# Moving the second expert stretch ahead of the last two head pairs, and spreading the VectorE side jobs over the cycles

## The reference

```
x = x + attn_a(layernorm(x))   # 16 heads of 16, ALiBi bias, causal, biases on q, k, v, o
x = x + ffn(layernorm(x))      # dropless experts, 8 experts, top 2
x = x + attn_b(layernorm(x))   # 16 heads of 16, rotary q and k, causal
x = x + ffn(layernorm(x))      # the same experts and the same routing
```

## Time and profile before

| what | value |
|---|---|
| time, median of 3 runs | 4382.41 us (4375.72 to 4391.83) |
| time of the profiled execution | 4379.86 us |
| its span, first to last instruction | 4378.1 us |
| mean granted TensorE clock | 0.967 |
| TensorE matmul busy | 4043.3 us, 92% |
| VectorE busy | 2996.7 us, 68% |
| ScalarE busy | 2815.2 us, 64% |
| GpSimd busy | 816.2 us, 19% |
| DMA, mean | 93 GB/s |

### The profile page before, as it was taken

How to read it: one execution, slowest core, us unless ns; L and a number is a source line. 1 busy time by engine, 2 the same in 40 slices (tenths; PEclk the granted TensorE clock), 3 DMA queues, 4 the chain that set the end, 5 groups by cost and what they waited for, 6 DMA issues and landing times.

```text
span 4378.1 us, 107651 instructions
## 1 busy us (share of the span) xinstructions
PE 4043.3 (92%) x42369; PEld 2482.4 (57%) x42369; DVE 2996.7 (68%) x3995; ACT 2815.2 (64%) x5843; POOL 816.2 (19%) x832
## 2 busy tenths in 40 slices
PE   5899999999999999998999999999999999998875
PEld 4455555555555555557855555555555555554764
DVE  4888887878877777880078888788888777773000
ACT  2377777777777776672257777777777777667211
POOL 3000001111111122330032222222232320111012
PEclk9799999999999999999989999999999999999987
DMA  5222233233333433335543333323423232221553
GB/s 175 49 61 61 61 78 80 64 77 98 75 72 77 106 83 91 96 90 178 189 110 94 86 87 99 93 72 91 113 75 92 76 90 57 59 56 61 160 172 116
DMA packets 247476, 407.05 MB, mean 93 GB/s; under 512 B 29325, under 2 KB 162189, under 8 KB 233869
## 3 DMA queue, kind: packets, MB, share of 16 engines
q1 hardware_dynamic: 243896, 391.76, 34.0%
q0 software_dynamic: 3072, 8.39, 0.6%
HBM read 264.25 MB, written 121.50 MB: 88 GB/s over the span
## 4 chain that ended last, share of the span: by engine, by line
PE 44%; DVE 5%; ACT 3%; issue 3%; DMA 2%; POOL 1%; SPq 0%; ACTq 0%; DVEq 0%; POOLq 0%
PE ps_acc L909 11%; PE ps_r L848 8%; PE ps_p L878 7%; PE ps_r L1001 5%; PE ps_p L990 4%; DVE part_max L1122 4%; ACT probs L730 3%; PE ps_r L948 2%; PE ps_r L956 2%; PE ps_r L952 1%; PE ps_r L853 1%; DMA hid_f<-rows_by_expert 1%; PE ps_p L872 1%; PE ps_p L885 0%; DVE xl L1083 0%
## 5 line engine op out<-in xcount | busy, mean ns | idle before, releaser
L1122 DVE TENSOR_REDUCE part_max<-ps_p 128x2 f32<-128x1024 f32 (+3 forms) x2560 | 2624.2, 1060 | 716.6 <-PE ps_p L878 530.2
L730 ACT ACTIVATE probs<-ps_r 128x512 f32<-128x512 f32 (+1 forms) x4608 | 2348.0, 574 | 724.4 <-PE ps_r L848 451.7
L848 PE MATMUL ps_r<-q_stack,k_stack 54*128 54x512 f32 (+3 forms) x5120 | 1381.2, 392 | 30.9 <-ACT probs L730 15.7
L878 PE MATMUL ps_p<-k_stack,q_stack 52*128 52x512 f32 (+3 forms) x5120 | 1243.1, 434 | 90.8 <-DVE part_max L1122 71.2
L909 PE MATMUL ps_acc<-probs,v_head 128*17 128x256 f32 x19456 | 1159.5, 364 | 1.2 <-ACT probs L730 1.2
L848 PEld LDWEIGHTS ps_r<-q_stack,k_stack 54*128 54x128 f32 x5120 | 733.5, 189 | 243.2 <-ACT probs L730 182.4
L878 PEld LDWEIGHTS ps_p<-k_stack,q_stack 52*128 52x128 f32 x5120 | 556.6, 189 | 418.1 <-DVE part_max L1122 237.4
L909 PEld LDWEIGHTS ps_acc<-probs,v_head 128*17 128x17 f32 x19456 | 492.5, 98 | 477.4 <-issue 226.3
L1198 DVE COPY xf<-ps_r 128x256 f32<-128x256 f32 x60 | 25.5, 424 | 460.0 <-PE ps_r L1001 460.0
L948 PE MATMUL ps_r<-xT,wqkv 128*128 128x256 f32 x1024 | 289.6, 409 | 17.4 <-ACT probs L730 14.5
L853 PE MATMUL ps_r<-id,mk 64*128 64x64 bf16 x3584 | 280.3, 195 | 0.0
(11 more groups left out here) (94 smaller groups left out, 2301.8 us busy)
## 6 DMA issues: line engine op xcount, KB each, us to landing
probs<-w_dram SPq DMA_DIRECT2D x60, 1024.0 KB, 8.3
q_stack<-parts SPq DMA_DIRECT2D x384, 128.0 KB
k_stack<-parts SPq DMA_DIRECT2D x384, 128.0 KB
parts<-pa SPq DMA_DIRECT2D x128, 256.0 KB, 2.5
parts<-pb SPq DMA_DIRECT2D x128, 256.0 KB, 3.5
o_sums<-acc_sb SPq DMA_DIRECT2D x1024, 17.0 KB
bk<-o_sums SPq DMA_DIRECT2D x64, 256.0 KB
bk<-recips SPq DMA_DIRECT2D x64, 256.0 KB
```

Source lines behind the costliest of these rows:

```text
L730: act.activation(probs[:, at % PBUF, u, 0:w], block_bank(g, n, u)[:, 0:w], ACT.Exp)\
L848: mm = pe.matmul(bank[:, col:col + QW - q0], ks[s][r, kb * P:(kb + 1) * P], qs[s][r, qt * QW + q0:(qt + 1) * QW], start=fresh, stop=True, ...
L878: mm[u] = pe.matmul(banks[:, u, col:col + w], qs[s][r, qb * P:(qb + 1) * P], ks[s][r, kc * QW:kc * QW + w], start=fresh, stop=True, skip_g ...
L1122: mm = dve.tensor_reduce(part_max[:, :, qb, kc], ps_p[:, p1_banks(g, n), col:col + w], AX_X, ALU.max)
```

## The change

The change has five parts. The second expert stretch is moved from behind pair 63 to behind pair 61 (`EX_AFTER`). The projection of batch 6, whose routed rows the stretch needs, is moved to earlier cycles of pairs 56 to 62 (`Y_ALONE`). The first two tiles' rows and the first tile's W1 are loaded already at step 30 of the pair before each stretch, W1 into the free buffer of the rows to be mixed (`first_rows`, `w1_first`); those rows are loaded later instead. Norm parts `ln` stand at the last step of a cycle, one per cycle; the mixing becomes 16 jobs, one per cycle from step 11 of the pair behind a stretch. The last batch is projected by query tile: jobs `zl` to `zo` load row sums, invert, store them, load, scale, project into `ps_p` and add on VectorE, for tile 3 inside pair 63, for tiles 2, 1 and 0 behind it. `AFTER_AT` and `AFTER_SP` go.

```diff
+Y_ALONE = (8, 11, 14, 17, 23, 26, 29, 32, 37, 39, 41, 43, 49, 51, 53, 55)
+EX_AFTER = (NG // 2 - 1, NG - 3)
+LAST = NB - 1
...
-        return [(t, ("ld", f, c, 0))] + [(t + 7 + 2 * i, ("ln", f, c, i)) for i in range(len(NORM_FROM))]
+        first = CYCLE * ((t + 7) // CYCLE) + CYCLE - 1
+        return [(t, ("ld", f, c, 0))] + [(first + CYCLE * i, ("ln", f, c, i)) for i in range(len(NORM_FROM))]
...
-            y_at = [slot_step(k) for k in Y_SLOTS[CH * c:CH * (c + 1)]]
+            y_at = [slot_step(k) for k in (Y_SLOTS if f is not None else Y_ALONE)[CH * c:CH * (c + 1)]]
...
-    if g == NG // 2:
-        for n, k in ((26, 0), (30, 1)):
-            steps[n].append(("fm", 0, 0, k))
-        steps[31].append(("fo", 0, 0, 0))
+    for ly in range(2):
+        for i in range(TOPK * NFT):
+            at = MIX_STEP + CYCLE * i
+            if g == EX_AFTER[ly] + 1 + at // STEPS:
+                steps[at % STEPS].append(("fm", ly, 0, i))
+    if g == EX_AFTER[0] + 2:
+        steps[STEPS - 1].append(("fo", 0, 0, 0))
+    if g == EX_AFTER[0] or g == EX_AFTER[1]:
+        steps[FETCH_STEP].append(("xw", EX_AFTER.index(g), 0, 0))
+    if g == NG - 1:
+        for n, job in LAST_JOBS:
+            steps[n].append(job)
...
+MIX_STEP, FETCH_STEP = 11, 30
+LAST_JOBS = ((19, ("zl", 3, 0)), (20, ("zc", 3, 0)), (20, ("zs", 3, 0)), (21, ("zb", 3, 0)), (22, ("zx", 3, 0)),
+             (23, ("zm", 3, 0)), (28, ("z", 3, 0)), (28, ("z", 3, 1)), (29, ("zl", 2, 0)), (30, ("zc", 2, 0)),
+             (30, ("zs", 2, 0)), (31, ("zb", 2, 0)), (31, ("zm", 2, 0)), (32, ("z", 3, 2)), (32, ("z", 3, 3)),
+             (34, ("za", 3, 0)), (34, ("za", 3, 1)), (34, ("za", 3, 2)), (34, ("za", 3, 3)), (34, ("zx", 2, 0)),
+             (35, ("zl", 1, 0)), (35, ("zc", 1, 0)))
...
+                elif kind == "zb":
...
+                    sp.dma_start(z_rows[c], rows_of(x_a, b, c)).then_inc(z_in[c], 16)
+                    for k in range(KD):
+                        sp.dma_start(z_o[c][:, k, :], o_d[f % 2, k * PAIRS:(k + 1) * PAIRS, 0:DH, cols]).then_inc(z_in[c], 16)
+                    sp.wait_ge(z_recip_st, 16 * (NQ - c))
+                    for k in range(KD):
+                        r = r_d[f % 2, k * PAIRS:(k + 1) * PAIRS, cols].rearrange("h (o n) -> h o n", o=1)
+                        sp.dma_start(z_rl[c][:, k, :], r.broadcast_to([PAIRS, DH, QW])).then_inc(z_in[c], 16)
...
+            def first_rows(ly):
...
+                for i in range(2):
+                    sp.dma_start(xs_sb[:, i, :, :], slots(xs, i)).then_inc(xs_in[i], 16)
+                e = sp.value_load(expert_of[0:1, 0:1], min_val=0, max_val=E - 1)
+                sp.dma_start(w1_first, w1[bass.ds(e, 1), :, :].rearrange("o (k p) f -> p (o k) f", p=P))\
+                    .then_inc(w1_first_in, 16)
...
+            job("zs", LAST, 1, 0)
+            store_o(NG - 1, 0)
+            job("zb", LAST, 1, 0)
+            job("zl", LAST, 0, 0)
+            job("zo", LAST, 3, 0)
+            job("zs", LAST, 0, 0)
+            job("zb", LAST, 0, 0)
+            job("zo", LAST, 2, 0)
+            job("zo", LAST, 1, 0)
             store_mixed(1)
+            job("zo", LAST, 0, 0)
...
+            def last_y(c, i):
+                n = CH * (NQ - 1 - c) + i
+                pe.wait_ge(z_scaled, KD * (NQ - c))
+                if n < 4:
+                    pe.wait_ge(p1_used, STEPS * NG)
+                else:
+                    pe.wait_ge(z_out, n - 3)
+                for k in range(KD):
+                    mm = pe.matmul(ps_p[:, n % 4, 0:D], z_o[c][:, k, i * P:(i + 1) * P], wo[:, k, :], start=(k == 0),
+                                   stop=(k == KD - 1))
+                mm.then_inc(z_mm, 1)
```

More of the change, by code:

```diff
@@ L378, in build @@
         o_scaled = sem("o_scaled")
-        y_out = sem("y_out")
+        z_sums = sem("z_sums")
+        z_recip = sem("z_recip")
+        z_recip_st = sem("z_recip_st")
+        z_in = [sem(f"z_in{c}") for c in range(NQ)]
+        z_bias = sem("z_bias")
+        z_scaled = sem("z_scaled")
+        z_mm = sem("z_mm")
+        z_out = sem("z_out")
+        w1_first_in = sem("w1_first_in")
         res_step = sem("res_step")
@@ L742, in value_evac @@
                     acc_evac(g, LAST_QT[GROUP_AT[k]])
-                if k == 0 and g % (NG // 2):
+                if k == 0 and g and g - 1 not in EX_AFTER:
                     acc_evac(g - 1, 0)
@@ L965, in value_slot @@
                     times_v(g, GROUP_AT[k])
-                elif k == 0 and g % (NG // 2):
+                elif k == 0 and g and g - 1 not in EX_AFTER:
                     times_v(g - 1, GROUPS - 1)
+            def last_y(c, i):
[3 more added lines that the diff above has]
+                    pe.wait_ge(p1_used, STEPS * NG)
+                else:
+                    pe.wait_ge(z_out, n - 3)
+                for k in range(KD):
+                    mm = pe.matmul(ps_p[:, n % 4, 0:D], z_o[c][:, k, i * P:(i + 1) * P], wo[:, k, :], start=(k == 0),
+                                   stop=(k == KD - 1))
+                mm.then_inc(z_mm, 1)
             def turn_slots(ly, i):
@@ L1003, in experts @@
                         mm.then_inc(fy_mm, 1)
-                    if ly:
-                        for j in AFTER_AT.get(i, []):
-                            job(*j)
                 pe.wait_ge(ys_out, 2 * ETILES * (ly + 1))
@@ L1039, in _ @@
                     score(g, n + 3, 1, masks_first=True)
-                if g % (NG // 2) == NG // 2 - 1:
+                if g in EX_AFTER or g == NG - 1:
                     times_v(g, GROUPS - 1)
-                    experts(g // (NG // 2))
+                if g in EX_AFTER:
+                    experts(EX_AFTER.index(g))
+            for c in (2, 1, 0):
+                for i in range(CH):
+                    last_y(c, i)
         @block.vector
@@ L1198, in experts @@
                         dve.tensor_copy(ys_sb[:, s, c, :], y_bank[c]).then_inc(ys_out, 1)
-                    if ly:
-                        for j in AFTER_AT.get(i, []):
-                            job(*j)
+                    if i == 1:
+                        dve.wait_ge(xb_in, 16 * (ly + 1))
+                        for t in range(NFT):
+                            dve.tensor_tensor(xb[:, t, :], xb[:, t, :], fb_bc[:, :], ALU.add).then_inc(mixed, 1)
             for n in range(STEPS):
@@ L1210, in _ @@
                         job(*j)
-                if g % (NG // 2) == NG // 2 - 1:
-                    experts(g // (NG // 2))
-            for k in range(TOPK):
-                mix(1, k)
+                if g in EX_AFTER:
+                    experts(EX_AFTER.index(g))
+            for c in (2, 1, 0):
+                for i in range(CH):
+                    job("za", LAST, c, i)
+                if c == 2:
+                    job("zx", LAST, 1, 0)
+                    job("zc", LAST, 0, 0)
+                elif c == 1:
+                    job("zx", LAST, 0, 0)
 def kernel(**inputs):
```

163 lines of the change are left out of this document (95 added, 68 removed).

## The result

The changed kernel takes 4284.8 us (median of 4 runs, 4281.91 to 4287.87) against 4380.7 for the kernel before, taken beside it (4 runs): a ratio of 0.9778, 95% interval 0.9757 to 0.9798, some 96 us less. Forecast were 4246 us, 134 us less; the time lies inside the stated range of 4212 to 4290, 5 us under its upper end. The profiled execution took 4282.6 us.

A forecast was written before the change was run, and what follows sets the result against it. Pairs cost what TensorE issues unless VectorE is late; in the stretches and the tail something else leads. Terms -12.9, -9, -42, -10, +3, -63 sum to -134 us: from 4379.9 to 4246 us, range 4212 to 4290.

The forecast's parts named there:

- rival C: Rival, chance 0.10: GpSimd's work delays 72 of 216 norm parts, taking back as much as spreading them wins; 4288 us.
- Part 1, the entry: Start of the expert stretches: with rows and W1 loaded before the pair ends, W2's matmuls start earlier; -12.9 us.
- Part 2, the mixing: Pair 32: the mixing's eight instructions in one step no longer close TensorE off for 6.7 us; -9 us.
- Part 3, the norm parts: Norm parts one per cycle: loss per batch 5 us (first layer), 17 (second), mostly from their bursts; 70% returns, -42 us.
- The sign for failure: The prediction fails if batch 5 keeps 459 us, tile 3's wait is absent, or a stretch opens waiting for a load.
- Part 4, batch 6 earlier: Second layer: new slots remove one of two places where SyncE's wait for the routed rows' norm delays later DMAs; -10 us.
- Rival E: Rival, chance 0.10: in SyncE's queue the step 30 fetch or pair 63's chain holds back another DMA; 4261, with two 4276.
- The +3: Pairs 26 to 30: norm parts now share cycles with routed norms, costing 3 us.
- Part 5, the end: From pair 63's TensorE end before the change to the span's end: second stretch shorter, tile chains added; 278.3 against 341.4, -63 us.
- A, short chains: Rival, chance 0.17: in the last batch five loads take 4 us, tile 3 is scaled in time, tail 30 us; 4222.
- B: Rival, chance 0.15: spreading the norm parts brings all, -65 instead of -42 us, with no GpSimd meetings that count; 4223.
- D, each part a stall: Rival, chance 0.02: norm parts at a cycle's last step delay the reduction TensorE needs next, each a stall; 4482 us.

The follow-up runs named there:

- the experiment: The changed kernel with tile 3's four projections and their additions moved from pair 63 to behind the pair: 4274.4 us, ratio 0.9772.

## Why the prediction was right, and where it was not

The direction held, and the size roughly (96 us for 134). That the time is inside the range is in part luck: the range reached up to 4290 for the sake of rival C at 4288, and C is not what happened. By the sum's own terms two of its six, -42 and -10, came to about -9 and 0.

**Part 1, the entry: right.** -13.1 us for -12.9, both stretches at 216.0 and 216.2 us, clock 1.00.

**Part 2, the mixing: right.** -10.1 for -9, and the wait of 6.7 us is gone.

**Part 3, the norm parts: wrong in size.** The step that failed is "Loss per batch: 5 in the first layer, 17 in the second", put down to the norm parts with 60 of 66 us. The first 5 was right: 3.6 to 4.1 us of them came back. Of the second layer's 17, some 10 go with GpSimd's three long instructions, with old and new steps alike. The sign for failure ("if batch 5 keeps 459 us") nearly came true: pairs 40 to 47 keep 457.7 us, some 5 of them through the wait for scaled rows in pair 40. Pair 42 has 59.4 us at clock 1.00, where "below 59" was written. The spreading is worth 17 to 37 us alone, about 9 within the change, and not 42.

**Part 4, batch 6 earlier: wrong.** "One of two such knots falls away" was the step; it moved by two pairs, worth nothing (0.9999). The argument had counted knots and had not followed which norm part each `bl` waits for. It had also put all 14.5 us of waits for the row of maxima down to the norm: 2.1 of them are in pair 0, 7.5 in pair 26, and only 4.9, in pair 58, in the second layer, so -10 was large even for a knot that goes. Rival E had named this kind of knot at 0.10. The +3 for norm parts that share cycles with routed norms didn't show: pairs 24 to 31 took 474.2 us before and 472.9 after.

**Part 5, the end: the sum right, -59.8 for -63, its working partly wrong.** TensorE's wait at step 28 was 10.9 us for 10.8, the tail 45.7 for 43.5. But the wait was charged as 14.8 us on the path, and the experiment shows that without it the tail grows by as much. Both numbers belong to one chain of SyncE's, stores, sums, reciprocals, loads of four tiles one behind the other. The reason given for tile 0's late reciprocal, the order on VectorE, was wrong too. The close numbers hide errors that cancel: over the four tiles the scaling started 7.9 to 9.8 us after the last load's issue (9.3 in the sum) and took 3.5 to 3.7 us (2.5), and tile 0's sums took 8.3 us to land where the sum has them ready.

**The rivals.** A, short chains, did not come: no tile's loads took 4 us, the four took 7.9 to 9.8. B did not come either. C gave 4288, next to the measured time, but by a sum that is not what happened: it let GpSimd take 72 us back from a gain that was never there. What GpSimd takes, it took before. D, each part a stall, is nowhere to be seen: TensorE's small waits for maxima fell from 129 to 102.

## What to carry to other kernels

A loss that is found by subtracting a good pair from a bad one belongs to everything in which they differ; take one candidate out on the chip before pricing an edit that removes another. When one queue issues all transfers in order, ask of each wait which of the transfers behind it needs it, and give that one a place of its own: the wait for a norm held four loads and the row of maxima that had nothing to do with it; cutting it out took away 22 us of TensorE's waits and brought 13 to 23 us on one chip, while on another the pairs stayed long for a reason that was not found. And an engine's wait near the end is only worth what the chain behind it gives up when it goes.
